# Weight loads of a five-stage hybrid layer: earlier issue, one semaphore per slice, a private cast buffer

## The reference

```python
x = x + mamba(layernorm(x))      # in_proj, conv over 4 tokens, SSM scan, gated norm, out_proj
x = x + ffn(layernorm(x))
x = x + attn(layernorm(x))       # 16 heads, rotary embedding, causal, 4096 tokens
x = x + ffn(layernorm(x))        # the same weights again

def ffn(x):
    x_prev = shift_by_one_token(x)
    xr = mu_r * x + (1 - mu_r) * x_prev
    xk = mu_k * x + (1 - mu_k) * x_prev
    r = sigmoid(xr @ W_r.T)
    k = square(relu(xk @ W_k.T))
    return r * (k @ W_v.T)
```

## Time and profile before

| | us |
|---|---|
| median of 2 runs | 9172.45 |
| lowest and highest | 9158.35 and 9186.54 |
| the profiled execution | 9237.24 |
| its span on core 1, the slowest | 9235.3 |
| spans of the 8 cores | 9184.5 to 9235.3 |

### The profile page before, as it was taken

How to read it: one execution, slowest core, us unless ns; L and a number is a source line. 1 busy time by engine, 2 the same in 40 slices (tenths; PEclk the granted TensorE clock), 3 DMA queues, 4 the chain that set the end, 5 groups by cost and what they waited for, 6 DMA issues and landing times.

```text
span 9235.3 us, 85272 instructions; the slowest of 8 cores (9184.5 to 9235.3 us)
## 1 busy us (share of the span) xinstructions
PE 4989.3 (54%) x21232; PEld 2049.1 (22%) x21232; DVE 3287.9 (36%) x6508; ACT 2354.5 (25%) x3568; POOL 149.0 (2%) x234
## 2 busy tenths in 40 slices
PE   0226647466464664255533655656666666744555
PEld 0213223232232323022211211211111222212222
DVE  0444453444444444355531332332221111114444
ACT  0113121231312313100010110134555765730111
POOL 2000000000000000000001000000000000000000
PEclk9556756566575665577766776767777888866666
DMA  6431201011010110201134222210000000011110
GB/s 95 104 106 36 62 1 63 24 40 57 6 63 27 36 53 10 46 37 37 37 69 87 66 74 72 65 51 33 33 33 33 1 33 33 1 32 42 44 40 37
DMA packets 338090, 419.97 MB, mean 45 GB/s; under 512 B 123041, under 2 KB 182946, under 8 KB 337570
## 3 DMA queue, kind: packets, MB, share of 16 engines
q1 hardware_dynamic: 248210, 360.00, 12.1%
q0 software_dynamic: 89424, 54.52, 3.8%
HBM read 331.39 MB, written 119.87 MB: 49 GB/s over the span
## 4 chain that ended last, share of the span: by engine, by line
PE 35%; DVE 23%; ACT 17%; DMA 11%; issue 10%; DVEq 1%; SPq 1%; POOL 1%; ACTq 1%; POOLq 0%
ACT pt_sb L191 11%; PE pEF L191 10%; PE pB L191 9%; PE pA L191 9%; PE pCD L191 7%; ACT D L191 3%; DVE y L191 2%; DVE t1b L191 2%; DMA wtmp<-win_l 2%; DVEq L189 1%; DMA xtm<-x 1%; ACT tr L191 1%; DMA wq_sb<-wqkv_l 1%; DVE xn L191 1%; DVE yraw L191 1%
## 5 line engine op out<-in xcount | busy, mean ns | idle before, releaser
L191 ACT ACTIVATE pt_sb<-pEF,ebias 128x1024 bf16<-128x1024 f32 (+1 forms) x640 | 631.2, 986 | 809.0 <-PE pEF L191 751.0
L191 PE MATMUL pA<-pt_sb,vb 128*65 128x512 bf16 (+3 forms) x1152 | 472.6, 410 | 425.1 <-ACT pt_sb L191 305.0
L191 ACT ACTIVATE pt_sb<-pCD,ebias 128x1024 bf16<-128x1024 f32 (+2 forms) x640 | 610.7, 954 | 115.6 <-PE pCD L191 32.7
L191 DVE TENSOR_TENSOR pt_sb<-pt_sb,mask01b 128x128 bf16<-128x128 bf16 x512 | 115.4, 225 | 1398.7 <-ACT pt_sb L191 1373.0
L191 PE MATMUL pB<-pt_sb,vb 128*65 128x512 bf16 (+3 forms) x1152 | 472.3, 410 | 35.2 <-DVE pt_sb L191 29.6
L191 PE MATMUL pA<-r_t,wr_sb 128*128 128x512 bf16 x512 | 147.2, 439 | 632.9 <-DVE h L191 632.9
L191 ACT ACTIVATE D<-pEF,cumcT 128x128 f32<-128x128 f32 x512 | 188.2, 368 | 851.8 <-PE pCD L191 815.2
L191 DVE TENSOR_TENSOR Gm<-E,Gmsk 128x1024 bf16<-128x1024 f32 x128 | 156.9, 1225 | 556.3 <-ACT E L191 556.3
L191 PE MATMUL pA<-xn,wq_sb 128*128 128x512 bf16 x768 | 228.2, 451 | 224.2 <-DMA wq_sb<-wqkvb_h 123.5
L191 ACT ACTIVATE sig_t<-pA 128x512 bf16<-128x512 f32 x64 | 38.2, 597 | 1135.5 <-PE pA L191 1135.5
L191 PE MATMUL pEF<-qq_sb,K_sb 64*128 64x512 bf16 (+1 forms) x1152 | 265.4, 430 | 63.9 <-DMA qq_sb<-q_hbm 63.4
(11 more groups left out here) (254 smaller groups left out, 8500.8 us busy)
## 6 DMA issues: line engine op xcount, KB each, us to landing
winm<-winb_h SPq DMA_DIRECT2D x272, 256.0 KB, 2.5
wq_sb<-wqkvb_h SPq DMA_DIRECT2D x192, 256.0 KB, 2.7
xrtB<-xres SPq DMA_DIRECT2D x16, 2048.0 KB, 8.7
xrtC<-xres SPq DMA_DIRECT2D x16, 2048.0 KB, 9.8
xtm<-x SPq DMA_DIRECT2D x32, 512.0 KB, 3.9
xres<-xcs SPq DMA_DIRECT2D x32, 512.0 KB, 2.9
xrt<-xres SPq DMA_DIRECT2D x8, 2048.0 KB, 10.9
xres<-xrt SPq DMA_DIRECT2D x8, 2048.0 KB, 6.9
```

The costliest lines, as they stand in the source:

```text
L191: ins = getattr(h, ent[1])(*ent[2], **ent[3])
```

## The change

Stage 0: `wdt_sb` is allocated and loaded ahead of the 35 casts, on a semaphore of its own; the loads of `woutb` alternate between two semaphores.

Stage B: the 24 weight loads are issued kc by kc (wr, wk, wv of one kc), on one semaphore for each kc, and the load of wk waits for that of wr, and wv for wk. The spreading of the mean no longer waits for the weights; in block 0 each matmul of R, K and V waits for its own slice.

Stage C: the casts go through a buffer of their own, `wtmpC`. In block 0 the load of slice m into `wq_sb` waits for the cast of slice m alone, in the projection's first block for that of slice 24 + mo. The loads of cos and sin stay behind the casts.

```diff
 # phase0
+    c.wdt_sb = c.stW.enter_context(nc.sbuf_tensor("wdt_sb", [128, NCH * 128], BF16)).ap()
+    w_wdt = S.dma("gpsimd", c.wdt_sb, kchunk_view(c.win_l[34]), ch="gw")
     st = {}
     with nc.sbuf_tensor("wtmp", [128, 2 * NCH * 128], BF16) as wtg:
...
     for kc in range(16):
-        w = [st[NMCH - 1], st[NMCH - 2]] if kc == 0 else []
+        w = [st[NMCH - 1], st[NMCH - 2]] if kc < 2 else []
         S.dma("gpsimd", c.woutb[:, kc * 1024:(kc + 1) * 1024],
-              c.wout[kc * 128:(kc + 1) * 128, :], ch="g0", waits=w)
-    c.wdt_sb = c.stW.enter_context(nc.sbuf_tensor("wdt_sb", [128, NCH * 128], BF16)).ap()
-    w_wdt = S.dma("gpsimd", c.wdt_sb, kchunk_view(c.win_l[34]), ch="g0")
+              c.wout[kc * 128:(kc + 1) * 128, :], ch="g%d" % (kc % 2), waits=w)
 # phaseB
-    for wsb, wsrc in [(wr_sb, c.wrT), (wk_sb, c.wkT), (wv_sb, c.wvT)]:
-        for kc in range(NCH):
-            w_wl = S.dma("gpsimd", wsb[:, kc * 1024:(kc + 1) * 1024],
-                         wsrc[kc * 128:(kc + 1) * 128, :], ch="bw")
+    w_wld = {}
+    for kc in range(NCH):
+        prev = []
+        for wi, (wsb, wsrc) in enumerate([(wr_sb, c.wrT), (wk_sb, c.wkT),
+                                          (wv_sb, c.wvT)]):
+            w_wld[(wi, kc)] = S.dma("gpsimd", wsb[:, kc * 1024:(kc + 1) * 1024],
+                                    wsrc[kc * 128:(kc + 1) * 128, :],
+                                    waits=prev, ch="bw%d" % kc)
+            prev = [w_wld[(wi, kc)]]
...
-        w = bgw(c, "C") + [ld_m] + ([w_wl, w_h1] if mg == 0 else [])
+        w = bgw(c, "C") + [ld_m] + ([w_h1] if mg == 0 else [])
...
+                wk2 = (w if kc == 0 else []) + \
+                    ([w_wld[(0, kc)]] if mg == 0 else [])
...
 # (the same for K with w_wld[(1, kc)] and for V with w_wld[(2, kc)])
 # phaseC
+    wtmpC = al1("wtmpC", [128, 2 * 1024], BF16)
...
-        sl = wq_sb[:, b * 1024:(b + 1) * 1024]
+        sl = wtmpC[:, b * 1024:(b + 1) * 1024]
...
-            w = ([w_win_used[gm - 3]] if gm >= 3 else []) + ([w_wcast, w_wcast2] if gm < 3 else [])
+            w = ([w_win_used[gm - 3]] if gm >= 3 else []) + \
+                ([st[m]] if mg == 0 else [])
...
-        w = [st_q] + (w_c1done if qm == 0 else []) + \
+        w = [st_q] + (w_c1done + [w_wcast, w_wcast2] if qm == 0 else []) + \
...
-            w = [w_wp_used[gm2 - 3]] if gm2 >= 3 else []
+            w = ([w_wp_used[gm2 - 3]] if gm2 >= 3 else []) + \
+                ([st[24 + mo]] if qm == 0 else [])
```

More of the change, by code:

```diff
@@ L1034, in phaseB @@
     w_ost = {}
-    for wsb, wsrc in [(wr_sb, c.wrT), (wk_sb, c.wkT), (wv_sb, c.wvT)]:
-        for kc in range(NCH):
-            w_wl = S.dma("gpsimd", wsb[:, kc * 1024:(kc + 1) * 1024],
-                         wsrc[kc * 128:(kc + 1) * 128, :], ch="bw")
+    w_wld = {}
[7 more added lines that the diff above has]
+            prev = [w_wld[(wi, kc)]]
+    w_wl = w_wld[(2, NCH - 1)]
     S.op("vector", "memset", h1, 0.0)
@@ L1102, in phaseB @@
                      r_t[:, kc * 512:(kc + 1) * 512],
-                     start=(kc == 0), stop=(kc == 7), waits=w if kc == 0 else [])
+                     start=(kc == 0), stop=(kc == 7), waits=wk2)
             w_rmm[mo] = S.ms("tensor")
@@ L1110, in phaseB @@
             for kc in range(NCH):
+                wk2 = (w if kc == 0 else []) + \
+                    ([w_wld[(1, kc)]] if mg == 0 else [])
                 S.op("tensor", "matmul", pb[bk][:, 0:512],
@@ L1134, in phaseB @@
                     w = (w0 + [w_ka[NCH - 1]]) if kc == 0 else []
+                if mg == 0:
+                    w = w + [w_wld[(2, kc)]]
                 S.op("tensor", "matmul", pb[bk][:, 0:512],
@@ L1269, in phaseC @@
         b = m % 2
-        sl = wq_sb[:, b * 1024:(b + 1) * 1024]
-        w = [st[22 + m]] if True else []
+        sl = wtmpC[:, b * 1024:(b + 1) * 1024]
+        w = [st[22 + m]]
         src = bass.AP(c.wproj.tensor, c.wproj.offset + m * 128,
```

## The result

| | before | after |
|---|---|---|
| median of the timed executions, us | 9228.9 (10) | 9070.45 (11) |
| lowest and highest | 9156.33 and 9293.52 | 8969.9 and 9103.89 |
| ratio, 95% interval | | 0.9808, 0.9754 to 0.9862 |
| the profiled execution, us | 9237.24 | 9116.06 |

So the change makes the kernel faster: 0.0192 x 9229 = 177 us, and 0.0202 x 9254 = 187 us in the second comparison. The plain medians differ by 158 us. The forecast was 200 us off a median of 9172, 8972, with a range of 8905 to 9045; the measured 9070 lies outside it.

The account below looks back on a forecast made before the run. No engine is full; three waits on weight loads (227.8, 212.5 and 127.4 us) stood out. Gains of 165 (stage 0), 26 (stage B) and 9 (stage C) made 200 us, off the median 9172.45: 8972, range 8905 to 9045.

Parts of the forecast that it names:

- I take the same 200 us off it: Whole kernel: the gain summed for the profiled execution (9237.24 us) was subtracted from the runs' median, 9172.45, giving 8972.
- Stage 0: forecast 165 us: Stage 0: the tile chain starts 227 us earlier and loses 61 to sharing DMA engines with casts and woutb.
- overlap with a price and not a queue: Stage 0: tiles run beside GpSimd's loads, about 3.0 us dearer each beside casts; woutb adds 6 us on two or three tiles.
- Rival (a): Stage 0: overlap with the casts is nearly free; total gain 262 us, time 8911; chance 0.17.
- Rival (b): Stage 0: deeper contention, every tile pays 6.9 us as on core 5; total gain 135 us, time 9037; chance 0.17.
- (e): Stage 0: tiles and casts shut each other out; slower beyond 14.9 us added per tile, about 9370 at 26; chance 0.02.
- Stage B: forecast 26 us: Stage B: a chain of 16 load waits, 4.5 us a link; V starts at 103 us, gaining 15.7 and 10.7.
- Rival (c): Stage B: the chain's links take 6.1 us and the stage loses 24 us; time 9022; chance 0.09.
- Stage C: forecast 9 us: Stage C: sin behind the casts keeps the stall under another name; m = 2's permutation comes 6 to 12 us earlier.
- (f): Stage C: the private buffer's full success would add some 110 us, excluded because cos and sin stand behind the casts.
- Rival (d): Stages 0 and B: VectorE delays each GpSimd issue by about one instruction, 17 us per stage B; time 9006; chance 0.04.
- The estimate of 215 us: Stage 0: by the skill page's figures, 86 GpSimd issues beside VectorE work cost 2.5 us more each.

Follow-up runs that it names:

- the second comparison: The unaltered changed kernel, e4, timed beside the kernel before (median 9253.92 us): ratio 0.9798.
- e4: The changed kernel unaltered, profiled and timed again beside the kernel before: median 9062.1 us, ratio 0.9798.
- e7: The changed kernel with SP issuing stage 0's x loads two tiles ahead of use: ratio to the kernel before 0.9651.
- e5: The changed kernel with stage B's loads each on its own semaphore, no GpSimd waits, all wr, then wk, then wv: median 9051.09 us, no ratio.
- e9: The changed kernel with stage B's loads kc by kc, each on its own semaphore, no GpSimd waits: ratio to the kernel before 0.9649, two executions.
- e3: The kernel before with only stage C as changed: median 9266.3 us, ratio 1.0021.
- e6: The changed kernel with cos and sin loads of blocks 0 and 1 issued ahead of stage C's casts: ratio to the kernel before 0.9656.
- e2: The kernel before with only stage B as changed: median 9239.48 us, ratio 0.997.

## Why the prediction was right or wrong

The forecast was 98 us too low. Two steps failed: the level that the gain was taken from (56 us), and, in stage 0, the price of woutb, taken as overlap where the runs show a queue. By the plain medians the gain was 42 us short of the 200, by the ratios 23 and 13.

**The level.** The larger failure is "I take the same 200 us off it": the working took the median of two executions, 9172.45, as the kernel's time. With ten and twenty-three executions the medians were 9229 and 9254. That alone moves the forecast from 8972 to 9029 or 9054, and with the range moved likewise 9070 would lie inside. The front table gave the warning: its profiled execution took 9237, above both. The range had terms for each unknown of the change and none for the level it was subtracted from.

**Stage 0: forecast 165 us, measured 153 (645.3 to 492.6) in the profile and 161 (to 484.7) in e4.** Beside the casts the mechanism was right, and the price per tile too: 15.8 forecast, 15.6 measured. Beside woutb "overlap with a price and not a queue" failed, and its term of 6 us was mis-sized. In after, core 1, one x load landed only with the last of woutb, after 20.9 us, and TensorE and VectorE waited up to 20 for it: that tile took 29.9 us (288.76 to 318.67), 17 more than 12.79. The 13 tiles behind it took 13.6 each, 10 us more in all, as their x loads still landed in 4.6 and not 3.9. So the tiles from 288.8 on lost 28 us where I had 6, and those beside the casts 47 where I had 55: 75 against 61. The longest landing before, 10.8, was no bound, because there no tile ran beside woutb.

**Rival (a)** (overlap nearly free) fell: x loads at 6.5. **Rival (b)** (every tile pays 6.9) fell as well: beside the casts a tile paid 2.8. **(e)**, tiles and casts shutting each other out, is refused by the tile of 15.6; yet e7 shows its beginning, as a faster tile chain made each cast 9.8 us.

**Stage B: forecast 26 us in two passes, measured 11 + 8 = 19.** The chain was named, and e5 and e9 show that it is the cause. Two of its terms were off. The first kc took 13.0 us and not 9.5, with xrtB in flight, for which I had allowed half a microsecond (no run takes xrtB out); the link itself, 9.8 per kc on core 1, was nearly right, but wr's landings beside wv of the kc before were longer than wk's (4.6 against 3.6, medians of after, core 1). K's wk[7] was thus in use 80.3 us after the first issue and not at 75.5. On core 1 V still started near the forecast, at 104.7 against 103, because the groups behind it took 24.4 us and not 27.1: in part luck. **Rival (c)**, a loss of 24 us, did not come: no core started V later than 113.3 in e4 against 116.6 at the earliest before. In the second pass cores differ more in the kernel before (113.2 to 127.5) than core 1's 113.7 told me.

**Stage C: forecast 9 us.** On core 1, m = 2's permutation moved by 18.3 - 7.0 = 11.3 us relative to sin's issue, inside the 6 to 12. From the stage's memset it moved by 7.1 in after, 6.5 in e3 and 8.0 in e4 (medians), as sin was issued 5 to 6 us later. In the length of stage C it is too small to be told. That the stall would only change its name was the firmest step, and the trace has it in one row: 106.38 us on sin_sb. e6 shows the cause, and its 105 us are the "some 110 us" of **(f)**.

**Rival (d)** and the rule behind it (the Trainium skill, "SBUF — State Buffer", section "Who interferes with whom"): it cost no time that can be told, but the traces agree that VectorE can block an issue. In stage 0 of after, 19 of 52 issues beside a TENSOR_SCALAR from SBUF were lengthened, by about the rest of that instruction at most, and in e7 one took 2.42 us beside an instruction of 2.34. In stage B, where (d) put its price, there is none: the 48 issues of core 1 took 528 to 551 ns, and the two of them that ran beside a TENSOR_SCALAR, one that reads PSUM, took 528. The estimate of 215 us from that page's figures is far too high here, since it let every issue meet such an instruction.

**The sum**: 165 + 26 + 9 = 200 against 177 and 187 by the ratios. The parts by marks give 153 to 161, 19 and about 7, that is 179 to 187.

## What to carry to other kernels

A wait that is removed pays only up to the next wait behind it on the path: before an edit, list for the instruction set free every operand and which queue brings it, and where in that queue it stands (sin behind 32 casts cost 105 us, by e6). Waits put into a DMA queue to share a semaphore turn overlapped loads into a chain of landings; a semaphore for each load in flight gave 20 to 26 us here in each pass. And a forecast of a time needs a term for the spread of the level that it is subtracted from, as well as for the change.

## What the runs showed of the hardware

Loads on SP's queue and casts on GpSimd's slow each other, and a faster chain of tiles slowed the casts further. A 256 KB cast cycle of 5.86 us alone became 7.5 beside tiles of 15.6 us and 9.8 beside tiles of 10.05, and a 512 KB x load went from 3.9 to 6.5 and 6.8. Behind 16 loads of woutb issued back to back it took 19 to 32.

The length of a stage with the same instructions depends on the clock that the core is granted in it. The busy times of stage A before on core 3 and then on core 1 (columns as in rows 5; the third number from the end is the granted clock):

```profile
672.30:3730.90 3058.60, 1735.77 (x9360) 887.76 (x9360) 1422.49 (x2649) 744.24 (x1512) 0.00 (x0) 0.65 0.12 38
...
676.00:3828.60 3152.60, 1822.56 (x9360) 909.19 (x9360) 1427.28 (x2650) 744.33 (x1512) 0.00 (x0) 0.62 0.12 37
```

Of the 94 us 87 are TensorE's: busy longer at 0.62 of full speed instead of 0.65, with VectorE's and ScalarE's busy times nearly the same. Over all 88 cores of the eleven profiles the length of stage A and its granted clock have a correlation of -0.98. In the profiles of e2 and e9 all eight cores stayed between 3058 and 3069 us; in others two to seven cores took 3077 to 3176, most often both cores of a pair (such as 4 and 5 before, 3116 and 3125). What decides which core it meets, no run here tells. It is as large as half the gain of this change. That it is also what moved the median of before is likely, not shown: no trace was kept of the executions timed beside it.
